# A graph layer on one core: the second norm's factors reach the taps' rows through DRAM instead of through matrix products, and two engines wait for constants one turn later

## The reference, cut to what matters

```python
def _bn(h, g, b, m, v):
    scale = g / jnp.sqrt(v + EPS)
    return h * scale[None, :, None] + (b - m * scale)[None, :, None]
h = _bn(_conv1d(xc, conv1_w, 0), bn1_g, bn1_b, bn1_m, bn1_v)
h = jax.nn.relu(h)
h = _bn(_conv1d(h, conv2_w, 8), bn2_g, bn2_b, bn2_m, bn2_v)     # 256 out x 256 in x 17 taps
x_conv = jnp.transpose(jax.nn.relu(h + xc), (0, 2, 1))
```

## Time and profile before

| | |
|---|---|
| median of 3 runs | 1787.47 us (1786.7 to 1787.77) |
| the profiled execution's own time | 1788.33 us |
| its span | 1786.5 us |
| PE busy | 1769.1 us (99% of the span) |
| DVE, ACT, POOL busy | 1211.5, 1000.4, 829.3 us |
| chain that ended last | PE 95%, issue 1%, DVE 1%, SPq 1%, POOL 1%, ACT 1% |

### The profile page before, as it was taken

The page is one execution under the profiler, slowest core; times in us unless marked ns, Lnnn a source line. Parts: engine busy times, 40 slices in busy tenths (PEclk is TensorE's granted clock), DMA queues, the critical chain, the costliest instruction groups (busy, mean ns, idle before and its releaser), DMA issues.

```text
span 1786.5 us, 30974 instructions
## 1 busy us (share of the span) xinstructions
PE 1769.1 (99%) x10778; PEld 1558.5 (87%) x10778; DVE 1211.5 (68%) x2318; ACT 1000.4 (56%) x1787; POOL 829.3 (46%) x988
## 2 busy tenths in 40 slices
PE   8999999999999999999999999999999999999998
PEld 7999999999999999999978888888888888888887
DVE  8999999999999847565654554544544545545545
ACT  6888888888888876665733332333332333333322
POOL 5788888887777637565721221221221212212211
PEclk9999999999999999999999999999999999999999
DMA  7566767676666454544763445435345344354442
GB/s 223 172 204 209 207 204 215 197 223 184 207 186 201 146 164 148 179 161 171 246 168 93 86 105 119 86 101 124 80 107 118 81 112 104 90 117 90 102 111 42
DMA packets 531865, 262.70 MB, mean 147 GB/s; under 512 B 366215, under 2 KB 494471, under 8 KB 531710
## 3 DMA queue, kind: packets, MB, share of 16 engines
q1 hardware_dynamic: 531166, 260.66, 52.2%
q10 hardware_dynamic: 544, 0.07, 0.0%
HBM read 151.58 MB, written 109.05 MB: 146 GB/s over the span
## 4 chain that ended last, share of the span: by engine, by line
PE 95%; issue 1%; DVE 1%; SPq 1%; POOL 1%; ACT 1%; DMA 0%; POOLq 0%; ACTq 0%; DVEq 0%
PE P L111 72%; PE P L612 6%; PE P L1016 4%; PE P L871 4%; PE P L641 4%; PE P L703 3%; PE P L660 2%; PE P L621 1%; SPq L946 0%; POOL axl L575 0%; SPq L920 0%; DMA yt<-y_d 0%; POOL af L572 0%; DMA x<-in_x 0%; DVE agl L417 0%
## 5 line engine op out<-in xcount | busy, mean ns | idle before, releaser
L998 POOL TENSOR_TENSOR xnx1l<-xnf,xnx1h 128x1024 fp32r<-128x1024 f32 x16 | 43.9, 2744 | 342.7 <-ACT xnx1h L991 342.7
L998 POOL TENSOR_TENSOR xnx0l<-xnf,xnx0h 128x1024 fp32r<-128x1024 f32 x15 | 41.5, 2770 | 319.3 <-ACT xnx0h L991 319.3
L1117 ACT ACTIVATE tr<-P,cold 128x512 f32<-128x512 f32 x64 | 44.2, 690 | 221.2 <-PE P L111 221.2
L1120 ACT ACTIVATE nn<-gn,col 128x512 f32<-128x512 f32 x64 | 46.4, 724 | 182.1 <-DVE gn L1141 182.1
L1137 DVE SCALAR_TENSOR_TENSOR gn<-tr,gn 128x512 f32<-128x512 f32 x64 | 44.3, 692 | 145.5 <-ACT tr L1117 145.5
L572 POOL TENSOR_TENSOR af<-af,at 128x512 f32<-128x512 f32 x64 | 110.0, 1719 | 42.9 <-ACT af L363 40.5
L575 POOL TENSOR_TENSOR axl<-af,axh 128x512 fp32r<-128x512 f32 x64 | 101.3, 1583 | 55.6 <-ACT axh L381 55.6
L1150 DVE SCALAR_TENSOR_TENSOR tz<-tz,tr 128x512 f32<-128x512 f32 x63 | 43.6, 692 | 120.3 <-ACT tz L1131 120.2
L612 PE MATMUL P<-ah,hd 128*128 128x256 f32 x512 | 122.3, 382 | 0.6 <-ACT hd L397 0.6
L1131 ACT ACTIVATE tz<-P,cold 128x512 f32<-128x512 f32 x63 | 43.4, 688 | 134.6 <-PE P L111 134.6
L111 PE MATMUL P<-w1mh,xxh 128*128 128x512 f32 x256 | 107.8, 421 | 0.0
(11 more groups left out here) (214 smaller groups left out, 6410.4 us busy)
## 6 DMA issues: line engine op xcount, KB each, us to landing
xh_d<-xst SPq DMA_DIRECT2D x64, 320.0 KB, 4.9
y_d<-yo SPq DMA_DIRECT2D x80, 256.0 KB, 2.1
yt<-y_d SPq DMA_DIRECT2D x128, 160.0 KB, 4.0
xl<-xh_d SPq DMA_DIRECT2D x36, 512.0 KB, 4.5
x<-in_x SPq DMA_DIRECT2D x64, 256.0 KB, 2.7
a<-in_adj SPq DMA_DIRECT2D x64, 256.0 KB, 3.0
at<-in_adjt SPq DMA_DIRECT2D x64, 256.0 KB, 4.2
x_d<-x SPq DMA_DIRECT2D x64, 256.0 KB, 4.4
```

What stands on the lines that cost most here:

```text
L998: e.e.tensor_tensor(o[1][:, :, :], xnf[p % 2][:, :, :, :].rearrange("p c i t -> p c (i t)"), o[0][:, :, :], ALU.subtract).then_inc(done, 1)
```

## The change

The factors of the second norm are written from `cold[:, 2:4]` to a DRAM tensor `s2_d` of 256 values, and seven DMAs read them back from there into `s2t`, one for each channel o within a block: 17 partitions get the same 37 (for the last three o 36) values, which lie 7 apart in DRAM. Two of the six diagonals, two products, two ACT copies, the table's seven columns and the two DVE operations go. ACT and POOL wait for the split weights before turn 6 and no longer before turn 5; `s2t` is waited for by POOL alone, where the first block is scaled.

```diff
+    s2_d = nc.dram_tensor("s2_d", (256,), F32, kind="Internal").ap()
...
-        tt_w = keep("tt_w", [119, 567])
+        tt_w = keep("tt_w", [119, 560])
...
@@ first_vector, first_gpsimd @@
-                e.wait_ge(S["normrow"], 2)
+                e.wait_ge(S["normrow"], 1)
...
-                e.wait_ge(S["s2t"], 2)
+                e.wait_ge(S["s2t"], 112)
...
@@ sync @@
             first_sync(e, 3)
+
+            e.wait_ge(S["consts"], 2)
+            sync.dma_start(s2_d.rearrange("(h p) -> p h", p=128), cold[:, 2:4],
+                           allow_slow_non_contiguous=True).then_inc(S["s2w"], 16)
             first_sync(e, 4)
             sync.dma_start(tt_w[:, :], ttab).then_inc(S["tt_in"], 16)
             first_sync(e, 5)
             sync.dma_start(ft[:, :], ftab).then_inc(S["ft_in"], 16)
+            e.wait_ge(S["s2w"], 16)
+            for o in range(7):
+                n = NW - 1 if 7 * (NW - 1) + o >= 256 else NW
+                rows = s2_d[o:7 * n + o - 6:7].unsqueeze(0).broadcast_to((17, n))
+                sync.dma_start(s2t[17 * o:17 * o + 17, 0:n], rows,
+                               allow_slow_non_contiguous=True).then_inc(S["s2t"], 16)
@@ scalar @@
-            for n, k in enumerate((0, 1, 4, 5, 2, 3)):
+            for n, k in enumerate((0, 1, 4, 5)):
...
-            e.wait_ge(S["rows"], 2)
-            scalar.copy(s2r[:, 0:256], P[CM0][:, 0:256])
-            scalar.copy(s2r[:, 256:7 * NW], P[CM0][:, 0:7 * NW - 256]).then_inc(S["normrow"], 1)
             first_scalar(e, 4)
+            first_scalar(e, 5)
 
             e.wait_ge(S["clo"], 3)
-            e.wait_ge(S["s2t"], 2)
-            for i in range(5, TURNS):
+            for i in range(6, TURNS):
@@ vector @@
-            e.wait_ge(S["normrow"], 2)
-            e.wait_ge(S["tt_in"], 16)
-            vector.tensor_tensor(s2m[:, :, :], s2r[0:119, :].rearrange("p (j o) -> p j o", o=7),
-                                 tt_w[:, 560:567].unsqueeze(1).broadcast_to((119, NW, 7)), ALU.mult).then_inc(S["s2t"], 1)
-            e.wait_ge(S["s2t"], 1)
-            vector.tensor_reduce(s2t[:, :], s2m[:, :, :], AX_X, ALU.add).then_inc(S["s2t"], 1)
             e.wait_ge(S["clo"], 3)
-            e.wait_ge(S["s2t"], 2)
@@ gpsimd @@
-            for i in range(2, 5):
+            for i in range(2, 6):
                 first_gpsimd(e, i)
             e.wait_ge(S["clo"], 3)
-            e.wait_ge(S["s2t"], 2)
-            for i in range(5, TURNS):
+            for i in range(6, TURNS):
@@ tensor @@
-            for n in range(2):
-                t = tensor.matmul(P[CM0][:, n * 128:n * 128 + 128], ones[:, :], diag[:, 4 + n, :],
-                                  start=True, stop=True, skip_group_check=True)
-            t.then_inc(S["rows"], 1)
             first_tensor(e, 4)
-            e.wait_ge(S["normrow"], 2)
+            e.wait_ge(S["normrow"], 1)
```

More of the change, by code:

```diff
@@ L67, in tap_table @@
             out[o, :, r // 20, r % 20, o] = v
-    of = np.repeat(np.eye(7), 17, axis=0)
-    return np.ascontiguousarray(np.concatenate([out.reshape(119, 560), of], axis=1).astype(np.float32))
+    return out.reshape(119, 560).astype(np.float32)
 class Place:
@@ L115 @@
 NAMES = """
-half one ident_in col_in eye2_in w0_in b0_in tt_in w1_in se_in bm_in ft_in gt_in tap0 tap1 s2t
+half one ident_in col_in eye2_in w0_in b0_in tt_in w1_in se_in bm_in ft_in gt_in tap0 tap1 s2w s2t
 consts crs diag rows normrow w1s chi clo ones taps
@@ L202, in gnn_kernel @@
         ones = stage("ones", [128, 128])
-        diag = stage("diag", [128, 6, 128])
+        diag = stage("diag", [128, 4, 128])
         s1r = stage("s1r", [128, 256])
-        s2r = stage("s2r", [128, 7 * NW])
-        s2m = stage("s2m", [119, NW, 7])
         ms = p1.hl("ms", [128, 2, 256])
```

## The result

The changed kernel takes 1813.55 us (median of 4 runs, 1812.08 to 1814.46) against 1787.62 us of before on the same chip (1786.7 to 1789.47): ratio 1.0144, 95% interval [1.0131, 1.0156], 25.9 us slower. The forecast was slower, 1834 us. The place and the kind of the loss are as forecast; its size is a little over half.

The account below looks back on a forecast made before the run. PE was taken as the bound, busy 1769.1 of 1786.5 us. The 46.5 us stall, swallowing the 1.6 us saving, on 1788.33 gave 1834.8 profiled, 1834 as median; the 8-in-10 range was 1800 to 1905.

Parts of the forecast that it names:

- The saving: At DVE's start of turn 5: 0.8 us of dropped operations and 0.8 us of idle time, 1.6 us in all.
- the stall: From ACT's copy to `xt` of graph 2 on, through DVE to PE: 46.5 us late, swallowing the 1.6 us saved.
- The write costs nothing: Writing 256 values to `s2_d` takes one SP issue, 0.4 to 0.6 us, in a gap of SP's: no cost.
- One engine, the same each time: Each 17-row load gets one DMA engine, all seven the same: 4352 packets in 54.8 us on it.
- the forecast's rival: Seven loads on seven different DMA engines, 7.9 us on each at 12.6 ns; at a low price, part of a 0.15 rival.
- 12.6 ns a packet: Price of each 4-byte element in the seven loads, taken from loads in 128 B runs: 54.8 us for 4352.
- the lower bound: Price line from 1 KB through 256 B down to 4 B: 6.3 ns a packet, 27.4 us of loads, 1806.6 us.
- 10.5 ns a packet: The skill's fixed price for each smallest-transfer packet: the seven loads would take 45.7 us, 9 us better than at 12.6 ns.
- Who waits: ACT's copy to `xt` of graph 2 waits for graph 1's store xn_d, landing at 89.7; `xxl` is 46.5 us late.
- The start at 30.8: Turn 5's backlog leaves the DMA engines by about 30.8 us, when the `s2t` elements begin, ending at 85.6.
- The clock, nothing to 2 us: PE's clock may begin low after the stall; PE has 2.2 us in hand, so nothing, up to 2 us if it lasts.
- 46.5: Lateness in us of DVE's `xxl` for graph 2, at 91.0 where it was at 44.50, kept for good by PE.

Follow-up runs that it names:

- mended kernel: The changed kernel with factors written 512 bytes apart, the seven loads spread over turns 5 to 9, and later buffers at their old places: 1790.24 us, ratio 1.0016.

## Why the prediction was right in kind, and 20 us too high

- **The saving** (1.6 us: half operations, half idle time): right in size at turn 5. Taking ACT's wait alone gave 0.9 us there, the operations too gave 1.6. In the change it is swallowed by the stall, as forecast; without the stall, the longer turns would still have taken 0.8 us of it, a term that the forecast didn't have.
- **The write costs nothing**: wrong. It was compared with a wait of SP 12 us later and not with the transfers behind it, which move half as much with it in flight. It costs 3.5 us alone, shown by taking it out and by moving its places apart.
- **One engine, the same each time**: the block of 27.3 us is there, and 16 + 1 rows took 18.3 us off, which speaks for one engine to a load. Whether it is the same one each time isn't shown. SP issues each load only when the one ahead is nearly through, so the seven would stand one behind the other on seven engines as well; the forecast's rival, by which each of seven engines would be held for a seventh of the time, left SP's issues out.
- **12.6 ns a packet**: the step that failed. It was made of a share, which counts overlapping packets twice, and of 128-byte runs. Read by count, 128 bytes cost 9.41 ns in such loads and 4 bytes 6.27: 27.3 us for 54.8. Of the error of 27.5 us, 4352 x 3.2 ns = 13.9 are the way of reading and 4352 x 3.1 = 13.6 the size. The forecast mixed two ways of reading: 12.6 came from a share, while 14.1 and 38 ns came from counts on full engines. Only by that mixture did the size seem to matter hardly at all below 256 bytes. The line through the two counts, which gave the lower bound, was the better guide: it has 6.3 ns at 4 bytes and 10.1 at 128.
- The 10.5 ns a packet that the Trainium skill ("DMA: Bandwidth & Descriptors", Bandwidth) has for its smallest transfer, issued by GpSimd, agree with neither number; by it the loads would have been 45.7 us, an estimate.
- **Who waits**: right, ACT's copy to `xt` of graph 2, behind it `xxh`, `xxl`, PE. But the store was to wait in the queue of one busy engine, with SP long done. In fact SP was held, the store went out at 61.62 only, and the piece from the last element to the copy was 66.13 - 60.6 = 5.5 us and not 4.1.
- **The start at 30.8**: 33.3. The earlier trace rows reads 30.5 rather than 30.8, and in the kernel after the transfers ahead were still being served, slowed by the write. In the mended kernel, with its write apart, nothing but elements moves from 31.2 on.
- **The clock, nothing to 2 us**: it did fall, and may have cost about 1.3. Stretches of the kernel after (PE, PEld, DVE, ACT, POOL busy, clock, DMA share, GB/s):

```profile
50.00:66.00 16.00, 0.00 (x0) 0.00 (x0) 0.00 (x0) 0.00 (x0) 0.00 (x0) 0.57 0.38 97
66.00:70.00 4.00, 0.61 (x3) 0.61 (x4) 2.56 (x6) 3.19 (x6) 0.00 (x0) 0.50 0.79 270
70.00:80.00 10.00, 10.00 (x59) 9.34 (x59) 8.54 (x23) 7.31 (x15) 6.49 (x12) 0.86 0.50 170
80.00:90.00 10.00, 10.00 (x66) 9.17 (x66) 7.54 (x21) 8.79 (x19) 7.09 (x11) 1.00 0.43 133
```

PE does nothing from 50 to 66 us, and the clock is at 0.50 (1.2 GHz) from 66 to 70 and back at 1.00 (2.4 GHz) by 80. `xxl` of turn 7 is 22.9 us late, that of turn 10 (98.43 for 74.23) 24.2; the difference is put down to the clock, by argument alone: no run here took it apart.

The sum again, by what was measured: 46.5 - 27.5 (price) + 2.5 (start) + 1.4 (end) = 22.9, as `xxl` has it; + 1.3 (clock) + 0.8 (longer turns) = 25.0; the span is 25.4 longer, the median 25.9. With the true price alone the forecast's sum would have been 1806.6, its lower bound, 7 us too low: part of the price's error covered terms that the sum put too low or at nothing. That is luck. By kernels: the change is 1.4 us above before without its small transfers, the write adds 3.5 and the loads 21.0, of whose 27.3 us 6.3 lie in time that nobody needed.

## What to carry to other kernels

Give a small transfer a number of rows that spreads, and not one like 17 (seven loads of 17 rows cost 18.3 us here against 16 + 1); if it can't be had, put a piece in each turn that is shorter than the slack there. Look at how long the issuing engine is held, and not only at the DMA engines. Price packets by their count over a stretch, not by the share of busy time. Ask of a small write what it does to the transfers behind it, and not only when it must have landed.

When a buffer changes its size, compare the length of a later turn in both traces before a gain or a loss is put down to anything else.

## What the runs showed of the hardware that was not expected

- 256 writes of 4 bytes side by side in DRAM: 9.2 to 9.7 us to landing, and 106 GB/s for 221 between 19 and 24 us; 512 bytes apart 3.8 us, as 128 pieces of 8 bytes 4.1 us (one run).
- In loads of 17 rows a 4-byte run passes each 6.27 ns and a 128-byte run each 9.41 ns; by share these read 8.9 and 12.9. In loads of 16 rows and 1 row the 4-byte runs pass each 2.2 ns.
- SP's issue itself waits behind such loads: 26.30 us for seven issues, where other issues of the kernel before take 0.4 to 0.6 us each, and the other transfers stand still meanwhile.
- A shift of all buffers by 32 bytes changed a turn of 9.833 us by 13 ns.
